# Making the 0/1 rows of the low source bits once per tile of edges instead of once per pair in the counting stage of a four-layer graph network

## The reference

```
norm = dis[src] * dis[dst]
h   = relu(segment_sum((x @ W1)[src] * norm, dst) + b1)
h   = relu(segment_sum((h @ W2)[src] * norm, dst) + b2)
out =      segment_sum((h @ W3)[src] * norm, dst) + b3   (+ x)
```

## Time and profile before

| | us |
|---|---|
| median of three runs | 7767.97 (7763.36 to 7768.62) |
| profiled execution, its own time | 7760.37 |
| profiled execution, span | 7758.3 |
| counting stage, first to last product | 2655.5 to 3623.0 |
| its 3920 matmuls, busy | 721.0 |
| its 980 `hot_joint`, busy | 670.4 |
| its 980 `hot_low`, busy | 248.7 |
| its 196 copies of a bucket (L2178), busy | 288.9 |

### The profile page before, as it was taken

How to read it: one execution, slowest core, us unless ns; L and a number is a source line. 1 busy time by engine, 2 the same in 40 slices (tenths; PEclk the granted TensorE clock), 3 DMA queues, 4 the chain that set the end, 5 groups by cost and what they waited for, 6 DMA issues and landing times. The chain is left out here.

```text
span 7758.3 us, 132909 instructions
## 1 busy us (share of the span) xinstructions
PE 6036.1 (78%) x34928; PEld 4270.5 (55%) x34928; DVE 4465.3 (58%) x13848; ACT 2998.7 (39%) x7877; POOL 4047.7 (52%) x4041
## 2 busy tenths in 40 slices
PE   7757627789967288665555566899999699999999
PEld 4326426788833144333454453799999444444444
DVE  9987915566644799765666666788888400000000
ACT  0001113445402136676666664788888100000000
POOL 7777767777677777402777771577777000000000
PEclk9877869999979699998777877999999899999999
DMA  1003312222230135665222224999999588788787
GB/s 46 3 7 94 98 51 55 55 55 55 52 95 18 25 102 181 192 204 161 53 53 53 53 53 113 359 380 388 384 383 374 188 294 293 289 295 291 290 304 266
DMA packets 531648, 1300.16 MB, mean 168 GB/s; under 512 B 107301, under 2 KB 332697, under 8 KB 498442
## 3 DMA queue, kind: packets, MB, share of 16 engines
q0 software_dynamic: 221568, 548.08, 21.5%
q1 hardware_dynamic: 114942, 568.32, 20.6%
q10 hardware_dynamic: 194700, 178.41, 7.1%
HBM read 1066.26 MB, written 228.24 MB: 167 GB/s over the span
## 5 line engine op out<-in xcount | busy, mean ns | idle before, releaser
L1979 PE MATMUL edge_p_m<-edge_rows,edge_onehot 128*128 128x128 f32 x9984 | 1128.5, 276 | 40.3 <-ACT edge_rows L1911 35.2
L201 POOL DMA_INDIRECT edge_rows<-tab,edge_slots x832 | 810.1, 974 | 664.0 <-DMA edge_slots<-slots_s 410.7
L1979 PEld LDWEIGHTS edge_p_m<-edge_rows,edge_onehot 128*128 128x128 f32 x9984 | 1121.0, 193 | 47.7 <-issue 28.7
L201 POOL DMA_INDIRECT edge_rows<-tab,pairs_pair_src x832 | 827.6, 995 | 504.5 <-issue 215.1
L2282 PE MATMUL conv_p_o<-conv_ring,acc_acc 128*128 128x512 f32 (+1 forms) x2548 | 1040.4, 570 | 32.4 <-DMA conv_roots<-dis_row 31.2
L1911 ACT ACTIVATE edge_rows<-edge_rows,edge_coef 128x128 f32<-128x128 f32 x3328 | 995.3, 387 | 166.8 <-DMA edge_rows<-tab,pairs_pair_src 166.8
L2165 PE MATMUL adj_cells<-adj_hot_joint,adj_hot_low 128*128 128x392 bf16 x3920 | 721.0, 334 | 402.0 <-SPq L2115 323.9
L208 POOL DMA_INDIRECT slots_s<-source_pays,source_row_s x782 | 839.3, 1073 | 284.0 <-issue 248.9
L577 POOL DMA_INDIRECT slots_d<-all_slots,pro_row_d x782 | 761.5, 974 | 270.9 <-issue 249.8
L982 POOL DMA_INDIRECT all_x<-tab_src,all_slots x784 | 742.2, 947 | 254.1 <-issue 238.6
L2282 PEld LDWEIGHTS conv_p_o<-conv_ring,acc_acc 128*128 128x128 f32 x2548 | 469.7, 191 | 585.8 <-issue 553.8
(11 more groups left out here) (455 smaller groups left out, 10027.5 us busy)
## 6 DMA issues: line engine op xcount, KB each, us to landing
conv_ring<-adjacency SPq DMA_DIRECT2D x252, 1792.0 KB, 7.2
adjacency<-adj_counts ACTq DMA_DIRECT2D x196, 784.0 KB
tab<-tab_o SPq DMA_DIRECT2D x50, 512.0 KB, 2.6
edge_rows<-tab,edge_slots POOLq DMA_INDIRECT x832, 2.5
edge_rows<-tab,pairs_pair_src POOLq DMA_INDIRECT x832, 5.9
tab_src<-all_x SPq DMA_DIRECT2D x50, 260.0 KB
tab_dst<-acc_acc SPq DMA_DIRECT2D x50, 260.0 KB
acc_acc<-tab_dst SPq DMA_DIRECT2D x50, 260.0 KB
```

Source lines behind the costliest of these rows:

```text
L201: pool.indirect_dma_start(out=rows[:, slot, j, :], out_offset=None, in_=table[:, :], in_offset=bass.IndirectOffsetOnAxis(ap=index, axis=0) ...
L1979: m = pe.matmul(at, onehot[:, z, j, :], rows[:, slot, j, b * H:(b + 1) * H], start=(n == 0), stop=(n == len(PARTS) - 1))
```

## The change

`hot_low` of a tile does not depend on the bucket. The change makes it once for each tile, four tiles with one instruction (`tensor_tensor`, 128 x 512, L2151 of the kernel after), and keeps it in a ring of 256 tiles (`LOWS`). The low bits are kept as bf16 for it (`low_b`). Pair n never needs a tile above n and never one below n - 195, so at the head of group g VectorE makes tiles 4g to 4g + 3, for the first 196 groups (`DG`). The new wait in front of it asks for the products up to pair 4(g + 1) - 60, and the wait of every `hot_joint` asks for the products up to n - 3, as before. TensorE now finds the place of `hot_low` by the pair's tile: it loads the packed words that VectorE uses, takes `word & 1` as the half of `cells`, and `(word >> 8) & 255` as the place in the ring. The count of matmuls, weight loads, `hot_joint` and everything of ScalarE and SyncE stay as they are.

```diff
--- before.py
+++ after.py
@@ -2085,13 +2085,15 @@
 def build_adjacency(nc, D, K):
 
 
-    HOTS, STAGES = 4, 2
+    HOTS, STAGES, LOWS = 4, 2, 256
+    assert LOWS >= REAL + 2 * G + HOTS
     with Scope(nc, "adj") as s:
         joint, low, rest = s.sb("joint", [P, DT]), s.sb("low", [P, DT]), s.sb("rest", [P, DT])
         high, block_of = s.sb("high", [P, DT], I32), s.sb("block_of", [P, DT], I32)
         offset = s.sb("offset", [P, VT])
         numbers = s.sb("numbers", [P, JOINT], F16)
-        hot_low, hot_joint = s.sb("hot_low", [P, HOTS, P], BF16), s.sb("hot_joint", [P, HOTS, JOINT], BF16)
+        low_b, hot_low = s.sb("low_b", [P, DT], BF16), s.sb("hot_low", [P, LOWS, P], BF16)
+        hot_joint = s.sb("hot_joint", [P, HOTS, JOINT], BF16)
         empty = s.sb("empty", [P, 4, BANK_COLS])
         counts = s.sb("counts", [P, STAGES, JOINT])
         cells = s.ps("cells", [P, 2, 4, 512])
@@ -2140,29 +2142,33 @@
             link(v.scalar_tensor_tensor(rest[:, :], joint[:, :], -float(P), rest[:, :], ALU.mult, ALU.add))
             link(v.scalar_tensor_tensor(joint[:, :], joint[:, :], float(SUB), slots[:, :, F_KEY], ALU.mult, ALU.add))
             link(v.scalar_tensor_tensor(joint[:, :], low[:, :], float(STEP_J - SUB), joint[:, :], ALU.mult, ALU.add))
-            link(v.tensor_copy(low[:, :], rest[:, :]))
+            link(v.tensor_copy(low_b[:, :], rest[:, :]))
 
             for g in range(VG):
                 words = load_registers(mybir.EngineType.DVE, REG_DVE, G * g, G, DT * 256 - 1)
+                if g < DG:
+                    wait(v, q["product"], G * (g + 1) + REAL - LOWS)
+                    v.tensor_tensor(hot_low[:, G * g % LOWS:G * g % LOWS + G, :], bcast_mid(K["iota_b"][:, 0:P], G),
+                                    bcast_last(low_b[:, G * g:G * (g + 1)], P), ALU.is_equal)
                 for j in range(G):
                     tile = (words[j] >> 8).with_bounds(min_val=0, max_val=DT - 1)
                     wait(v, q["product"], G * g + j - HOTS + 1)
-                    v.tensor_scalar(hot_low[:, j % HOTS, :], K["iota_b"][:, 0:P], low[:, ds(tile, 1)], None, ALU.is_equal)
                     v.tensor_scalar(hot_joint[:, j % HOTS, :], numbers[:, :], joint[:, ds(tile, 1)], offset[:, G * g + j:G * g + j + 1],
                                     ALU.subtract, ALU.is_equal).then_inc(q["hot"], 1)
 
         @block.tensor
         def _(pe):
             for g in range(VG):
-                buckets = load_registers(mybir.EngineType.PE, REG_PE, 2 * G * g + G, G, BUCKETS - 1)
+                words = load_registers(mybir.EngineType.PE, REG_DVE, G * g, G, DT * 256 - 1)
                 for j in range(G):
                     n = G * g + j
-                    half = (buckets[j] & 1).with_bounds(min_val=0, max_val=1)
+                    half = (words[j] & 1).with_bounds(min_val=0, max_val=1)
+                    place = ((words[j] >> 8) & (LOWS - 1)).with_bounds(min_val=0, max_val=LOWS - 1)
                     if n % 2 == 0:
                         pe.wait_ge(q["allowed"], n // 2 + 1)
                     pe.wait_ge(q["hot"], n + 1)
                     for c in range(4):
-                        m = pe.matmul(cells[:, ds(half, 1), c, 0:BANK_COLS].rearrange("p a c -> p (a c)"), hot_low[:, j % HOTS, :],
+                        m = pe.matmul(cells[:, ds(half, 1), c, 0:BANK_COLS].rearrange("p a c -> p (a c)"), flat(hot_low[:, ds(place, 1), :]),
                                       hot_joint[:, j % HOTS, c * BANK_COLS:(c + 1) * BANK_COLS], start=False, stop=True, skip_group_check=True)
                     m.then_inc(q["product"], 1)
```

## The result

The changed kernel takes 7957.11 us (median of 4 runs, 7953.76 to 7961.99) against 7765.66 us for the kernel before on the same chip (7757.85 to 7768.62): 1.0246 times as long, 95% interval 1.0233 to 1.0258. That is 191 us slower; the forecast of 7924 us is 158 above that median.

A forecast was written before the change was run, and what follows sets the result against it. TensorE and VectorE were taken as nearly level in the counting stage; 0.28 us a pair on TensorE gave +109 us early and +25, +15, +10, +5 later, +164 on 7760.4, so 7924 us; 8 in 10 range 7795 to 8005.

The forecast's parts named there:

- The two are nearly level: Counting stage, early: VectorE needs 3.04 us for a group of four pairs, TensorE 3.08, so neither waits much.
- The price of a register instruction: Before a pair's first matmul on TensorE: two ALU and one ISA add 0.28 us a pair in full; chance 0.62.
- the first stretch: First 395 us of the counting stage, 480 pairs: at 1.05 us a pair 504 us, +109.
- The lower end: Rival: only the added instructions' busy time counts on TensorE's sequencer, 0.11 us a pair, 7803 us; chance 0.15.
- the upper end: Rival: the added TensorE instructions cost the full 0.39 us a pair, 8003 us; chance 0.11, shared with a lower clock.
- the group of 3.08 us: TensorE's time for four pairs before the change: 2.67 us of matmuls plus 0.41 at the group's head.
- The 1.12: Addition to a TensorE group of four pairs, 4 x 0.28 us, taking it from 3.08 to 4.20.
- The later stretches by buckets: Four stretches after the first 395 us, summed by buckets of three, four or five pairs: +25, +15, +10, +5 us.
- The ring of copy and product with its chained pair: Late buckets alternate ScalarE and TensorE; copies 3.34 and 4.52 us apart; with three pairs only the chained pair grows, +0.14.
- VectorE's part at nothing: VectorE's group falls from 3.04 to 3.00 us, which does not enter the sum because TensorE becomes slower.
- The queue hides it.: Rival: TensorE's sequencer works ahead of the array, a pair stays at 0.77 us, time 7760 us; chance 0.07.
- Three marks: Expected profile signs: hardly any TensorE wait for `hot_joint`, VectorE waiting over 100 us, PE issue idle in nearly every pair.

The follow-up runs named there:

- the ladder: Runs changing TensorE's REGISTER_ALU per pair: none or one more in the kernel before, three more in the changed kernel; 7720.29, 7823.57 and 8197.88 us.
- experiment 2: The kernel before with VectorE's part of the change alone; TensorE takes a fixed matrix as weights and the old bucket words; 7760.41 us, ratio 0.9994.
- experiment 1: The kernel before with only TensorE's register instructions of the change (also called kernel 1), `hot_low` still made per pair; 7970.35 us, ratio 1.0266.
- experiment 3: The kernel of experiment 1 with rings of eight `hot_low` and `hot_joint` instead of four; 7971.12 us, ratio 1.0271.
- kernel 6: The kernel before without REGISTER_ALU on TensorE; one VectorE instruction makes all halves before the loop, TensorE loads four per group; 7720.29 us, ratio 0.9952.
- kernel 4: The changed kernel with place and half of all pairs worked out by two VectorE instructions; TensorE loads eight registers a group; 7775.08 us, ratio 1.0016.

## Why the prediction was right, step by step

- **What bounds.** "The two are nearly level" held. Taking one ALU away from TensorE gave 0.047 us a pair until VectorE's 0.76 stopped it at 0.774; adding one cost 0.081 at once. There was no slack for the additions.
- **The price of a register instruction.** Forecast 0.28 us a pair for two ALU and one ISA, from spacings of 0.10, 0.10 and 0.08. Measured in the first stretch 1.098 - 0.821 = 0.277, and 0.094 for an ALU in the ladder. The lower end, 0.11 by the busy times, is refuted by all four steps of the ladder: each costs more than its instructions are busy. So is the upper end, 0.39: each costs less than 0.13 us an instruction.
- **The sum is short by 26 us of 190, and nearly all of it is in one term, the group of 3.08 us.** The first stretch was forecast at 504 us and took 527. A group was put at 4.20 us, 3.08 for now and 1.12 more; it takes 4.39. The 3.08 is a group with a register load of 0.33 us, the median. But the stretch of the earlier trace rows had 395/120 = 3.29 us a group: by its own terms the prediction gives 370 us for it, and compared 504 from those terms with 395 as measured. Most of what 3.08 leaves out are the long register loads, which rows of the kernel before have already (up to 966 ns in the earlier trace rows). The 120 loads of the first stretch took 0.50 us on average before the change and 0.43 after it (median 0.34 and 0.33), and across a head the pairs start 1.21 us apart on average before, where the median is 1.07, and 1.52 after, where it is 1.43. The 1.12 was right: the group grew by 4.39 - 3.29 = 1.11. Added to the measured pace the 0.28 makes 480 x 0.28 = +134 us, and +132 were measured. In the terms of 4.20 itself, the loads are 0.43 - 0.33 = 0.10 of the missing 0.19, and nearly all the rest, 4 x 0.02, is the step behind an ISA, which is 0.10 us and not 0.08: the FUSED_REGOPS of the earlier trace rows had begun at 3502.08, before its window.
- **The later stretches by buckets.** Forecast +25, +15, +10 and +5; measured +23, +14, +14 and +6. The ring of copy and product with its chained pair was the right picture; the copies start as in the earlier trace rows, the chained wait is now 1.44 us instead of 1.14, which is the 0.28 and a little:

```profile
3717.05 1.48 ACT L2184 ACTIVATE adj_counts<-adj_cells 128x1568 f32<-128x1568 f32 x1 [1.44 <-PE adj_cells L2171]
...
3720.38 1.46 ACT L2184 ACTIVATE adj_counts<-adj_cells 128x1568 f32<-128x1568 f32 x1
```

- **VectorE's part at nothing.** Right by experiment 2, within 0.16%. The instruction of 512 columns takes 685 ns, as the float32 row did:

```profile
L2151 DVE TENSOR_TENSOR adj_hot_low<-all_iota_b,adj_low_b x196: 679/685/741, 2660.4 to 3547.0; 128x512 bf16<-128x512 bf16 x196
```

The Trainium skill's rule (VectorE: DVE Perf Modes, What auto-detection actually checks) that an operand with step zero keeps a 16-bit `tensor_tensor` at one column a cycle agrees: at the 0.96 GHz of the same page (Side-by-side: where the cycles go for N=2048 bf16) 512 columns are 533 of the 685 ns, an estimate.

- **"The queue hides it."** Refuted by experiment 1: with everything else unchanged the additions cost 205 us. The sequencer is not ahead of the array here: each matmul has a FUSED_REGOPS of its own, the loads of a pair start 0.125 us apart, and with the ALU and the waits a pair took the sequencer 0.63 and 0.70 us, where the array needs 0.67.
- **Three marks were off.** I said that TensorE would hardly wait for `hot_joint` any more. The profile puts 66.9 us of the first stretch down to it, and experiment 3 shows that this is an attribution and no wait that costs. VectorE's wait was to be over 100 us and is 94.3, and idle time of PE by "issue" was to stand in nearly every pair and stands in 126 places of 480 pairs. The stage is 1158 us long, 28 over the 1130 of the forecast, for the reason above. The other marks hold: 2940 ALU_OP and 4900 FUSED_REGOPS, the spacings of 0.9 and more, 1.4 at a head, and `hot_low` 196 times at 0.685 us.

```profile
L2171 PEldq FUSED_REGOPS  x4900: 46/46/46, 2662.1 to 3818.8; - x196
...
L2171 PEldq ALU_OP  x2940: 32/36/47, 2661.9 to 3818.4; - x196
```

A version that beats both kernels came out of the ladder: kernel 6, the kernel before with the halves worked out once, 0.9952 and again 0.9945 times the time of before.

## What to carry to other kernels

Count the sequencer's instructions beside the engine's: a matmul with an address from a register has a price in front of it that the busy times do not show, and it is read from the starts of neighbouring instructions. Here, where the sequencer is level with the array, moving an index computation into data, once, on an engine that makes all of it in one instruction, gained 41 us, and saving VectorE's work gained nothing. A wait that the profile infers can be a coincidence of two engines in lockstep; counting which matrix the waiting pair needs, and lengthening the ring between them, tells. And a model of a loop is first held against the time that the loop takes now: 3.08 against 3.29 us was there to be seen.

## What the runs showed of the hardware that I had not expected

- The same register load of four words takes 0.33 us mostly and up to 0.97 at times on TensorE's sequencer (0.34 to 0.38 and up to 0.99 on VectorE's); eight words take 0.59, so 0.064 us for each further word, and up to 1.75.
- A place and a half that come ready from memory need one FUSED_REGOPS together in front of the first matmul (3920 in kernel 4, busy 46 ns mostly and 88 at most), while worked out from a word they need two FUSED_REGOPS and three ALU_OP.
- GpSimd's scatter instructions took 1364 ns on average in the first stretch of kernel 6 (1218 in its repeat) and 959 with VectorE's part of the change added, while VectorE's own 1568-column instructions went from 679 (675) to 709.
- A register instruction costs TensorE's sequencer about 0.10 us from start to start, though it is busy for 32 to 46 ns; one that was busy for 14 ns longer (kernel 1) put its pair 14 ns later.
